# One block of a vision tower with routed experts on one core: loads and tile embedding in another order at the start, the last steps of the tile pipeline in an order of their own, six early routed slots

## What is computed

```python
h = patches(x) @ W_tok.T + b_tok                      # 768 -> 192
h = h + attention(layernorm(h))                       # 12 heads of 16, rope, causal over 16 tokens
t = rmsnorm(layernorm(h)) * scale
top_vals, top_idx = top_k(t @ gate_w.T + gate_b, 4)   # 4 of 16 experts
route_w = softmax(top_vals)
h1 = t @ mlp1_w[e].T + mlp1_b[e]                      # 192 -> 768
a = min(glu, 7) * sigmoid(1.702 * glu) * (clip(lin, -7, 7) + 1)   # glu, lin: even and odd columns
y = a @ mlp2_w[e].T + mlp2_b[e]                       # 384 -> 192
out = h + layernorm(h) + sum over the 4 experts of route_w * y
```

## Time and profile before

| | us |
|---|---|
| device time, three executions | 476.03, 477.01, 483.92 |
| median | 477.01 |
| the profiled execution | 478.07 |
| its span (first to last instruction) | 476.10 |
| around the span | 1.97 |

### The profile page before, as it was taken

How to read it: one execution, slowest core, us unless ns; L and a number is a source line. 1 busy time by engine, 2 the same in 40 slices (tenths; PEclk the granted TensorE clock), 3 DMA queues, 4 the chain that set the end, 5 groups by cost and what they waited for, 6 DMA issues and landing times.

```text
span 476.1 us, 14730 instructions
## 1 busy us (share of the span) xinstructions
PE 433.4 (91%) x3878; PEld 384.0 (81%) x3879; DVE 295.6 (62%) x1018; ACT 313.3 (66%) x816; POOL 244.1 (51%) x290
## 2 busy tenths in 40 slices
PE   3679899999999777999999999999999999999990
PEld 2457677767777555889999999999999999999990
DVE  0347888898889975855555555555555555555550
ACT  1047788778877945557677667766776677667740
POOL 2024557777777757632433545644454444553464
PEclk9589999999999955999999999999999999999997
DMA  8765656767585214245233344543343444433233
GB/s 231 172 182 162 191 161 179 199 192 213 165 236 182 73 50 125 101 101 108 48 53 63 63 62 63 78 69 52 54 71 61 60 60 62 64 43 36 26 34 33
DMA packets 41722, 49.73 MB, mean 104 GB/s; under 512 B 6387, under 2 KB 32995, under 8 KB 41668
## 3 DMA queue, kind: packets, MB, share of 16 engines
q1 hardware_dynamic: 27028, 33.93, 26.6%
q0 software_dynamic: 14640, 15.16, 20.1%
HBM read 30.83 MB, written 18.23 MB: 103 GB/s over the span
## 4 chain that ended last, share of the span: by engine, by line
PE 66%; DVE 14%; issue 8%; POOL 5%; ACT 2%; POOLq 1%; SPq 1%; DMA 1%; ACTq 0%; DVEq 0%
PE bank L545 24%; PE bank L579 15%; PE bank L559 13%; PE bank L533 3%; PE bank L461 3%; POOL routed_rows L1329 2%; PE bank L480 2%; PE bank L481 2%; PE bank L455 2%; DMA b_sb<-b 1%; DVE sc L962 1%; DVE rope_s L942 1%; POOL p_pair L1365 1%; DVE stats L1014 1%; DVE xn L929 1%
## 5 line engine op out<-in xcount | busy, mean ns | idle before, releaser
L545 PE MATMUL bank<-rT,w_now 128*128 128x128 f32 x948 | 124.4, 281 | 1.1 <-ACT rT L729 1.1
L545 PEld LDWEIGHTS bank<-rT,w_now 128*128 128x128 f32 x948 | 114.9, 193 | 6.9 <-ACT rT L729 1.8
L767 ACT ACTIVATE k_spread<-bank,w_now 128x128 f32<-128x128 f32 x237 | 70.0, 372 | 57.4 <-PE bank L559 55.9
L729 ACT ACTIVATE w_now<-w_sb 128x1158 f32 x79 | 92.2, 1170 | 16.6 <-issue 7.6
L1413 POOL DMA_INDIRECT out_rows<-x_sb,row_to x40 | 63.0, 1575 | 71.9 <-issue 25.5
L1108 DVE TENSOR_TENSOR v_sb<-bank,w_now 128x384 f32<-128x384 f32 x79 | 44.0, 557 | 76.9 <-PE bank L559 57.9
L579 PE MATMUL bank<-w_sb,p_spread 128*128 x474 | 83.8, 327 | 0.4 <-DVE half_s L1131 0.4
L1329 POOL DMA_INDIRECT routed_rows<-packet,row_i x64 | 64.0, 1001 | 30.5 <-PE bank L524 16.2
L579 PEld LDWEIGHTS bank<-w_sb,p_spread 128*128 128x128 f32 x474 | 76.1, 190 | 0.9 <-issue 0.8
L1121 DVE SCALAR_TENSOR_TENSOR p_spread<-k_spread,v_sb 128x384 f32<-128x384 f32 x79 | 44.1, 559 | 33.1 <-ACT k_spread L767 29.6
L559 PE MATMUL bank<-rT,w_now 64*128 64x128 f32 x948 | 64.2, 281 | 0.0
(11 more groups left out here) (222 smaller groups left out, 646.6 us busy)
## 6 DMA issues: line engine op xcount, KB each, us to landing
x_sb<-patches SPq DMA_DIRECT2D x16, 384.0 KB
w_sb<-w SPq DMA_DIRECT2D x32, 192.0 KB
w_sb<-w SPq DMA_DIRECT2D x16, 288.0 KB
w_sb<-w SPq DMA_DIRECT2D x64, 48.0 KB
wtok_sb<-routed_rows SPq DMA_DIRECT2D x25, 106.0 KB, 2.0
out_rows<-h SPq DMA_DIRECT2D x16, 96.0 KB
routed_rows<-zero_row SPq DMA_DIRECT2D x13, 106.0 KB
x_sb<-routed_rows SPq DMA_DIRECT2D x10, 106.0 KB
```

What stands on the lines that cost most here:

```text
L545: last = mm(dst[:, c * P:(c + 1) * P], w[:, a:a + P], t[:, part, :], start=(start and c == 0), stop=(not start and c == ICH - 1))
L729: return nc.scalar.activation(dst, src, ACT.Copy)
L767: last = nc.scalar.activation(gate_act[b][:, a:a + P], ps_glu[b][:, a:a + P], ACT.Silu, bias=w1_now[b][:, GLU_B + c:GLU_B + c + 1], scale= ...
```

## The change

Three parts of the program change.

**The start.** SP loads the embedding's bias under a semaphore of its own right behind the embedding weights, and the patches of tile 1 ahead of the attention weights; the first expert's load comes behind the patches of tile 2. PE embeds tiles 0 and 1 in step 0 and tile n at the beginning of steps n = 2 to 5 (`FILLING` = 6); DVE adds and measures them first in those steps. The wait for the small loads goes to step 2 on PE, and the scaling of the norm's weights to the end of step 1 on DVE.

The core of the diff:

```diff
-EARLY, EARLY_TILES = 4, 10
+EARLY, EARLY_TILES = 6, 10
...
+FILLING = 6
...
+        def weights_of(j, buf):
+
+            return w1_now[j % 3 if isinstance(j, int) and j < EARLY else buf % 2]
+
+        def rows_of(j, buf):
+
+            if isinstance(j, int) and j in (2, 3):
+                return (xnT_all[:], yT[:, 0:2, :])[j - 2]
+            return rT[buf % 2][:]
...
             sp.dma_start(x_sb[0][:], x[0]).then_inc(x_in[0], 16)
             sp.dma_start(wtok_sb[:], w_tok).then_inc(wtok_in, 16)
+            sp.dma_start(btok_bc[:], b_tok.to_broadcast([P, DIM])).then_inc(btok_in, 16)
             sp.dma_start(cst[:], consts).then_inc(consts_in, 16)
-            sp.dma_start(btok_bc[:], b_tok.to_broadcast([P, DIM])).then_inc(wsmall_in, 16)
+            sp.dma_start(x_sb[1][:], x[1]).then_inc(x_in[1], 16)
             sp.dma_start(wqkv_sb[0:HALF], w_qkv).then_inc(wqkv_in, 16)
             sp.dma_start(wqkv_sb[HALF:HALF + 1, 1, :], b_qkv).then_inc(wqkv_in, 16)
+            sp.dma_start(nscale_bc[:], nscale.to_broadcast([P, DIM])).then_inc(wsmall_in, 16)
...
-            load_x(1, 1)
-            load_expert(0)
             for t in range(2, 8):
                 load_x(t, t % 2)
-                load_expert(t - 1)
+                load_expert(t - 2)
+            load_expert(6)
...
             def first_end(j, buf):
+                pe.wait_ge(r["rT_ready"], 4)
+                first_whole(j, buf, True, (1,))
                 first_rest(j, buf, False).then_inc(r["first_done"], 1)
 
...
+                elif n == TILES + 2:
+                    drain_turn(last - 2)
+                    drain_ranks(last - 3)
+                    drain_project(last - 1)
+                    bank_free(("k_spread_ready", TILES))
+                    turn(ps_b1, b1_sb[:], ident[0:2 * ICH * EXPERTS, 0:2 * ICH * EXPERTS]).then_inc(b1_turned, 1)
+                    pe.wait_ge(early_step, EARLY_STEPS)
+                    for i in range(4):
+                        turned = mm(ps_etab[:, i * EARLY:(i + 1) * EARLY], of_early[0:EARLY, i:i + 1],
+                                    ident[0:EARLY, 0:EARLY], start=True, stop=True)
+                    turned.then_inc(early_turned, 1)
+                    drain_values(last)
+                    drain_weights(last - 3)
+                    drain_project(last)
+                    drain_gate(last - 2)
+                    drain_bias(last - 3)
...
+                if TILES < n < TILES + 4:
+                    return drain(n)
                 par = n % 2
+                if 1 < n < FILLING:
+                    bank_free(("h0_ready", n))
+                    embed(n, par, 16 * (n // 2 + 1))
...
+                    if tile(5) == TILES - 1:
+                        bank_free(("yT_ready", TILES))
+                        turn_early(1)
...
-                if tile(0) is not None:
+                if tile(0) is not None and n >= FILLING:
...
-                if isinstance(tile(0), int) and tile(0) == 0:
+                    embed(t, par, 16 * (t // 2 + 1))
+                if n == 0:
+                    embed(0, 0, 16)
+                    bank_free(("h0_ready", 1))
+                    embed(1, 1, 16)
...
-                    pe.wait_ge(wsmall_in, 16 * 7)
                     pe.wait_ge(setup_pool, 3)
                     pe.wait_ge(setup_act, 2)
+                if n == 2:
+                    pe.wait_ge(wsmall_in, 16 * 6)
                     pe.wait_ge(setup_dve, 3)
...
-            turn_early(1)
             first_layer(2, 2, True)
+            first_layer(3, 3, False)
...
             second_early(0)
+            pe.wait_ge(r["rT_ready"], 2)
+            turn_early(2)
+            first_layer(4, 4, True)
+            pe.wait_ge(table_ready, 1)
+            pe.wait_ge(pad_to_ready, 1)
             second_early(1)
+            first_layer(5, 5, False)
+            for j in range(2, EARLY):
+                second_early(j)
...
             def copy_w1(j, buf, expert):
-                wait(act, r["first_done"], j - 1)
-                wait(act, r["gate_ready"], j - 1)
-                wait(act, r["lin_ready"], j - 1)
-                copy(w1_now[buf % 2][:], w1_sb[:, bass.ds(expert, 1), :].rearrange("p a f -> p (a f)")
+                over = j - 2 if isinstance(j, int) and j < EARLY else j - 1
+                wait(act, r["first_done"], over)
+                wait(act, r["gate_ready"], over)
+                wait(act, r["lin_ready"], over)
+                copy(weights_of(j, buf)[:], w1_sb[:, bass.ds(expert, 1), :].rearrange("p a f -> p (a f)")
                      ).then_inc(r["w1_ready"], 1)
...
+                elif n == TILES + 2:
+                    turn_y(last - 1)
+                    turn_t()
+                    spread_probs(last)
+                    turn_y(last)
+                    turn_comb()
+                else:
+                    turn_t()
+                    turn_comb()
+                    if n == TILES + 4:
+                        act.wait_ge(s["proj_done"], TILES)
+                        turned_early(1)
+                        early[2] = expert_of(2)
+                        copy_w1(2, 2, early[2])
...
+                if n == TILES + 2:
+                    act.wait_ge(early_ready, 1)
+                    act.wait_ge(setup_dve, 5)
+                    act.wait_ge(experts_in, 16 * LOADS_E * EXPERTS)
+                    for j in range(2):
+                        early[j] = expert_of(j)
+                        copy_w1(j, j, early[j])
...
+            def scale_norm():
+                dve.wait_ge(wsmall_in, 16 * 6)
+                V.tensor_scalar(nscale_bc[:], nscale_bc[:], T_SCALE, None, ALU.mult).then_inc(setup_dve, 1)
+                dve.wait_ge(setup_dve, 3)
...
+                if n > TILES + 1:
+                    at(6, place_all)
+                    at(6, place_chosen)
+                    at(6, place_sum)
                 if n == TILES + 2:
                     early_table()
...
                     early_done()
-                at(0, embed_add)
-                at(0, embed_stats)
+                    first_biases()
+                    at(4, norm2)
+                    attn_add(TILES - 1)
+                    attn_stats(TILES - 1)
+                    attn_aggr(TILES - 1)
...
+                if n == 1:
+                    scale_norm()
...
             tab(13, V.tensor_tensor, left[:], cnt[:, 0:EXPERTS], inside[:], ALU.subtract)
+            linear(1, 1)
+            product(0, 0)
...
-                    scatter(now, 0, 2 if n < TILES + 2 else TOPK)
+                    scatter(now, 0, 2)
+                if n == TILES + 3:
+                    scatter(late, 2, TOPK)
...
+                    if not (known and j == EARLY):
+                        if b % ADDS > 0:
+                            owed = pool.value_load(table_i[0:1, 2, bass.ds(j, 1)], min_val=ADDS_FROM, max_val=16 * SLOTS)
+                        if b % ADDS < ADDS - 1 and not (known and j < ADDS):
+                            owed_wrap = pool.value_load(table_i[0:1, 3, bass.ds(j, 1)], min_val=ADDS_FROM, max_val=16 * SLOTS)
+                        alone(pool)
                     pool.wait_ge(r["row_to_ready"], j + 1)
                     pool.wait_ge(r["y_out_ready"], j + 1)
-                    pool.wait_ge(added[b % ADDS], ADDS_FROM if isinstance(j, int) and j < ADDS else owed_to(j - ADDS, b))
+                    pool.wait_ge(added[b % ADDS], ADDS_FROM if known and j < ADDS else owed_to(j - ADDS, b))
...
-                        if b % ADDS > 0:
-                            owed = pool.value_load(table_i[0:1, 2, bass.ds(j, 1)], min_val=ADDS_FROM, max_val=16 * SLOTS)
-                        if b % ADDS < ADDS - 1 and not (isinstance(j, int) and j < ADDS):
-                            owed_wrap = pool.value_load(table_i[0:1, 3, bass.ds(j, 1)], min_val=ADDS_FROM, max_val=16 * SLOTS)
```

263 lines of the change are left out of this document (158 added, 105 removed).

## The result

The changed kernel took 473.99 us (median of 20, 471.19 to 478.10) against 478.86 for the kernel before in 20 executions beside it (476.03 to 483.92). The ratio is 0.990, with a 95% interval of 0.988 to 0.992: 4.7 us faster, just under 1%. 472.6 had been forecast, from the first three executions of before, whose median was 477.01; the forecast gain was 4.4. The profiled execution of the changed kernel has a span of 471.8 us, where the sum had 471.7.

A forecast was written before the change was run, and what follows sets the result against it. PE was taken as the bound, busy 252.42 of 252.68 us in the long part. Span 476.10 - 4.9 (start) + 1.4 (drain, early slots) - 0.9 (tail) = 471.7, or 472.6 in median terms; range 466.0 to 477.8.

The forecast's parts named there:

- The start: Up to the turn of step 6: reordered loads, waits and embeddings give 4.9 us, bounds 0.2 and 7.0.
- The first rival: Start: PE's clock stays at half to about 22 us, 475.7, or later steps return the gain, up to 477.3; chance 0.22.
- The drain: From the pipeline's end to the first routed slot: the first slot begins 1.2 us later.
- the 3.46 us for ACT's copies: Drain: two copies of first weights ahead of tile 13's exponential add 3.46 us to the chain to the first slot.
- The early slots: From the first slot on: a stall of 1.7 us, less 0.86 of idle time and 0.67 of half-clock loss.
- The stall: Ahead of slot 4's first layer, PE waits 1.7 us for ACT's copy of turned rows, bounds 0 and 3.1.
- The 0.67 for half-clock products: First routed slot: beginning only the glu half there may save half of the 1.33 us lost at half clock.
- The idle time that I took as gone: Early slots: PE's 0.86 us of idle time goes, since rows 2 and 3 are turned early.
- the mark of 215.91: Early slots: slot 6's old start, 213.79, plus 2.12 for second layers 4 and 5, as the time to compare with.
- The tail: Last adds: POOL's loads moved ahead of its waits give 0.9 us; the loads' price was put at 1.14.
- The pass-through of the projection: Drain: tile 15's earlier projection makes the first slot 3.6 us earlier, 467.8 in all; chance 0.27.
- The clock that comes back late in the early slots: Early slots: PE's half clock costs 2.0 us a slot, 9.0 with four and a half slots, 481.6; chance 0.05.

The follow-up runs named there:

- FILLING = 4: Changed kernel with the embedding at the head of steps 2 and 3 alone, mid-step from step 4 on; ratio 0.984 to the kernel before, 471.3 us.
- the swap of two lines: Changed kernel with ACT copying the turned rows of slots 4 and 5 ahead of slot 5's first weights; ratio 0.989 to the kernel before.
- the run with both repairs: Changed kernel with embedding heading only steps 2 and 3, and slots 4 and 5's turned rows copied before slot 5's first weights; ratio 0.987, seven of ten executions.

## Why the prediction was right, point by point

**The start.** The total was well met: 4.9 forecast, 4.77 at step 6 and 4.47 behind it measured. So were its parts: first turn 12.81 for 13.2, second 17.68 for 18.3, turn of step 6 at 53.47 for 53.3. That steps 2 to 5 would give 2.05 back (35.0 us for 32.95) was forecast, and 2.84 were (35.79), for the reason given: the embedding delays a turn whose tile is ready. What I put as one average over four steps was one gain (1.3 in step 2, which had begun at half clock before), 0.8 lost in step 4 and one large loss, 3.5 us in step 3, of which 1.9 by the order and 1.6 by a clock that fell in this execution; with `FILLING = 4` the first part was avoidable. That the sum met the turn of step 6 within 0.2 is partly luck: from the first turn to that of step 6 the same start took 39.0 to 42.3 us in six traces, and 40.1 had been forecast. The patches of tile 1 were taken to be hidden. In the first trace they were; in four of the six traces they end PE's wait ahead of the second embedding, at 0.8 to 1.6 us. The first rival, the clock at half to 22 us, did not come in this execution: the stretch from 12 to 22 us that had been at 0.50 ran at 1.00, and the run with loads and waits alone shows the other case, q and k at half clock without the second embedding ahead of them. It did come in one of the nine traces with the second embedding there, the profiled one of the run with both repairs.

**The drain.** This step failed, in sign: 1.2 later was forecast and 0.77 earlier measured. The term that failed is the 3.46 us for ACT's copies ahead of tile 13's exponential. They were hidden, since DVE's operand came 0.90 later still: the gate of tile 13 now stands behind the projection of tile 15. The run with the copies back in step 19 shows it, where the exponential does not move. The exponential moved by 2.59 against the last turn (178.09 - 152.61 = 25.48, now 176.21 - 148.14 = 28.07), for that reason and not for the copies. The way from it to the first slot became 3.36 shorter (11.75 to 8.39), where I took 2.26 off for the projection.

**The early slots.** +0.17 was forecast (1.7 - 0.86 - 0.67), +1.45 measured up to slot 8. The stall was right, in its cause and nearly in its size: 1.45 for 1.7, and it went with the swap of two lines. The 0.67 for half-clock products was wrong: both halves of the first slot were slow, and in the eight other traces of the new order the 24 short products behind them, too (2.42 to 2.93 us, 1.63 in the first trace). So the first trace is the mild case: on the second chip the way from the first slot to slot 8 took 33.3 to 33.9 us in the three traces with the stall in it. The idle time that I took as gone partly came back where the long part begins, and the mark of 215.91 hid this. These two errors, 2.0 in the drain and 1.3 here with opposite signs, are why the sum of both, +1.4 forecast and +0.68 measured, looks better than its terms; and that the whole came out at -4.35 for -4.4 is luck, since no part did so well by itself.

**The long part and the tail.** The long part was to be unchanged and cost 0.33. The tail was to give 0.9; 0.58 came from the adds and 0.31 from the last pair, which I had not thought of. The 1.09 at the first of the last adds is the 1.14 of the sum; it shrinks on its way because a later add waits for its own data.

**The rivals.** The pass-through of the projection had 0.27 and is partly what happened, 0.77 of its 3.6. Its projection did end 3.5 us earlier, counted from the last turn (26.31 for 29.81), but the chain went through the gate of tile 13 behind it. The clock that comes back late in the early slots had 0.05. In its mechanism it is the usual case with the new order, eight of nine traces (24 products at 2.42 to 2.93 for 1.63 us), but over little more than part of one slot and not four: the price is 0.8 to 1.3, not the 4.4 that would outweigh the gain. The upper end of the range, 477.8, lies 0.3 above what its terms give with nothing kept of the start (472.6 + 4.9).

## What to carry to other kernels

A gap that an engine spends waiting costs twice where its clock is down behind it: with ready work moved into the gap the start gave 3.8 us, while taking away the wait alone gave 0.8. Move only as much ahead as the wait there has room for. The embeddings of tiles 2 and 3, ahead of turns that had waited 2.0 and 1.1 us, changed nothing by the move (36.6 us from the first turn to that of step 6, and 36.7 without); those of tiles 4 and 5, ahead of turns that had waited nothing and 0.6, cost 2.4 more (39.0, all with the clock at 1.00). An average over steps hides this. For a stage in which one tile goes round four engines, follow the one instruction from whose operand the next waits, also through what was put ahead of it on the other engine; and compare at a place where both kernels have the same work left.

## What was new about the hardware

The first turn of one and the same start moves between executions, from 12.29 to 14.29 us in six traces, with the landing of the embedding's weights and of the patches of tile 1 and with the second embedding's length (2.19 to 3.58 us). How often PE's clock falls behind it moves too: for the changed kernel and those that share its start, the way from the first turn to that of step 6 took 39.0 to 42.3 us in six traces.

At the start the granted clock and the rows don't always agree. In the first trace of the kernel before, q and k at 1.65 us stand in a window of 0.50; in its second trace, in the run with loads and waits alone and in the one with both repairs they take the same 1.65 us, and the windows read 1.00. What is called half clock in these three is read from the lengths of the rows.

Two of the three chips of the experiments show DVE waits around the last ranks that the trace ends with "remote", up to 6.5 us long, and PE waits of 0.5 to 2.9 us without a releaser beside them, in every kernel, the one before among them; the traces of the second chip and of the first comparison show no such DVE wait, and none of these PE waits around the last ranks. Their cause stays open: no experiment here separates it. The routed part of the kernel before is 3.8 us longer in the trace from such a chip, some 1.3 of it by the clock. That the waits lengthen it is read from where they stand, not tested. If so, they make a drain in which every engine waits for the next more costly than one trace from a chip without them tells.
